# Attention scores in four 32-row groups instead of two 64-row groups, and a two-trip loop written out, in a one-core decoder layer

## The reference

```
inter  = einsum('bhcd,bhde->bhce', qi * q_decay, kv)
scores = einsum('bhcd,bhsd->bhcs', qi, ki) * dmask
intra  = einsum('bhcs,bhse->bhce', scores, vi)
kv_new = r_C * kv + einsum('bhcd,bhce->bhde', ki * k_decay, vi)
```

## Time and profile before

| | |
|---|---|
| median of 3 runs | 180.23 us (179.91 to 180.83) |
| profiled execution, first to last instruction (span) | 178.7 us |
| PE busy | 152.3 us (85%) |
| DVE busy | 126.4 us (71%) |
| ACT busy | 61.8 us (35%) |
| POOL busy | 35.9 us (20%) |
| mean granted TensorE clock | 0.971 |

### The profile page before, as it was taken

The page is one execution under the profiler, slowest core; times in us unless marked ns, Lnnn a source line. Parts: engine busy times, 40 slices in busy tenths (PEclk is TensorE's granted clock), DMA queues, the critical chain, the costliest instruction groups (busy, mean ns, idle before and its releaser), DMA issues.

```text
span 178.7 us, 3036 instructions
## 1 busy us (share of the span) xinstructions
PE 152.3 (85%) x983; PEld 106.6 (60%) x983; DVE 126.4 (71%) x396; ACT 61.8 (35%) x171; POOL 35.9 (20%) x54
## 2 busy tenths in 40 slices
PE   0399964797997999999959999999599889998991
PEld 0267433573662678867626888677258757745880
DVE  0633599647487995975789959757899565877762
ACT  3346880103487132054751320547613220311110
POOL 3104163013161002222410013125100113010020
PEclk9999996569999999999999999999999999999999
DMA  5999200000200000000004000000010000001001
GB/s 173 290 360 340 57 0 4 0 0 2 69 10 0 0 4 0 0 2 0 0 4 132 0 0 0 0 0 0 0 59 0 4 2 0 0 0 59 4 0 59
DMA packets 7930, 7.29 MB, mean 41 GB/s; under 512 B 2264, under 2 KB 7664, under 8 KB 7792
## 3 DMA queue, kind: packets, MB, share of 16 engines
q1 hardware_dynamic: 7424, 6.79, 12.1%
q10 hardware_dynamic: 496, 0.37, 0.7%
HBM read 6.11 MB, written 1.05 MB: 40 GB/s over the span
## 4 chain that ended last, share of the span: by engine, by line
PE 43%; DVE 33%; issue 7%; ACT 6%; DVEq 5%; POOL 3%; DMA 2%; POOLq 0%
PE bank L784 15%; PE ebank L784 11%; DVE probs L613 9%; PE bank L894 4%; POOL rs L325 3%; DVE b_e_parts L738 3%; DVE stats L519 2%; ACT qx L425 2%; PE ebank L792 2%; DMA xin<-in_x 2%; DVE norm L530 2%; DVEq L520 2%; PE bank L799 2%; DVE acc L557 2%; PE bank L890 1%
## 5 line engine op out<-in xcount | busy, mean ns | idle before, releaser
L613 DVE TENSOR_TENSOR probs<-bank,dec 128x512 f32<-128x512 f32 x32 | 19.8, 683 | 1.9 <-PE bank L852 1.9
L852 PE MATMUL bank<-qx,kT 64*128 64x512 f32 x64 | 18.4, 625 | 0.7 <-ACT kv L480 0.7
L325 POOL TENSOR_TENSOR rs<-ve,nhalf 128x2 f32<-128x2 f32 x16 | 11.4, 711 | 36.6 <-DVE ve L524 36.5
L877 PE MATMUL bank<-probs,vpad 128*32 128x128 f32 x256 | 10.8, 293 | 4.1 <-DVE probs L613 4.1
L799 PE MATMUL bank<-cst,norm 128*128 128x128 f32 x36 | 6.4, 301 | 9.1 <-DVE norm L530 9.1
L784 PE MATMUL ebank<-w_e_hi,h3T_hi 128*128 128x512 f32 x40 | 13.3, 413 | 0.0
L557 DVE SCALAR_TENSOR_TENSOR acc<-ebank,gate,acc 128x256 f32<-128x256 f32 x26 | 11.3, 477 | 2.5 <-PE ebank L784 2.3
L425 ACT ACTIVATE qx<-bank,cst 128x256 f32<-128x256 f32 x32 | 12.6, 489 | 0.0
L557 DVE SCALAR_TENSOR_TENSOR acc<-bank,gate,acc 128x256 f32<-128x256 f32 x22 | 9.3, 478 | 4.5 <-PE bank L784 3.0
L784 PE MATMUL ebank<-w_e_hi,h3T_lo 128*128 128x512 f32 x40 | 12.5, 393 | 0.0
L784 PE MATMUL ebank<-w_e_lo,h3T_hi 128*128 128x512 f32 x40 | 12.4, 392 | 0.0
(11 more groups left out here) (135 smaller groups left out, 332.8 us busy)
## 6 DMA issues: line engine op xcount, KB each, us to landing
w_e<-in_L_ffn_We SPq DMA_DIRECT2D x2, 1024.0 KB, 10.8
xin<-in_x SPq DMA_DIRECT2D x4, 256.0 KB, 3.6
dec<-in_decay SPq DMA_DIRECT2D x1, 1024.0 KB, 7.9
out<-outb SPq DMA_DIRECT2D x8, 128.0 KB, 1.7
cst<-in_consts ACTq DMA_DIRECT2D x1, 282.0 KB, 3.6
w_qkv<-in_L_attn_Wq SPq DMA_DIRECT2D x1, 256.0 KB, 4.2
w_qkv<-in_L_attn_Wk SPq DMA_DIRECT2D x1, 256.0 KB, 4.6
w_qkv<-in_L_attn_Wv SPq DMA_DIRECT2D x1, 256.0 KB, 4.9
```

Source lines behind the costliest of these rows:

```text
L325: nc.gpsimd.tensor_tensor(dst[:], src[:], nhalf[:], ALU.pow).then_inc(done, 1)
L613: nc.vector.tensor_tensor(probs[:, t, 4 * n:4 * n + 4, :], bank[2 + n][:].rearrange("p (h n) -> p h n", h=4), dec[:, 4 * n:4 * n + 4, :], ...
L852: pe.matmul(bank[2 + n][:], kT[rows, t, g, :], qx[rows, t, g, :, :], start=True, stop=True).then_inc(s_sc_ps, 1)
L877: mm = pe.matmul(bank[t][32 * q:32 * q + 32, g * P:(g + 1) * P], vpad[:, t, h, :], probs[:, t, h, :], start=(par == 0), stop=(par == 1 and ...
```

## The change

The four row groups of the array that hold two heads each take the place of the two that hold four. `qx` has two masked copies (even and odd heads) instead of four. A product of `scores` takes 32 rows of kT and 256 columns of `qx`, and there are eight for a tile: for g = 0 one from each row group q into the left half of bank 2+q, then for g = 1 into the right half. The semaphore steps only after the g = 1 product of a bank, and `scores(1)` waits for bank 2+q ahead of its g = 0 product. A bank so holds heads of both groups; the decay table is permuted to match, and `attend` reads `probs` through the new order and takes all its waits in its first four products. Apart from that the loop of passes 2 and 3 is written out, and a dummy product of 512 columns becomes two of 256.

```diff
@@ shape_constants
-    c[:, C_PICK:C_BLOCK] = (head_of_row[:, None] % 4) == np.arange(4)[None, :]
+    c[:, C_PICK:C_BLOCK] = (head_of_row[:, None] % 2) == np.arange(2)[None, :]
...
-    decay = np.where(diff[:, None, :] >= 0, r[None, :, None] ** np.maximum(diff, 0)[:, None, :], 0.0)
+    order = [g * 8 + q * 2 + a for q in range(PAIRS) for g in range(GROUPS) for a in range(2)]
+    decay = np.where(diff[:, None, :] >= 0, r[None, order, None] ** np.maximum(diff, 0)[:, None, :], 0.0)
@@ decoder_layer
-        qx = sb("qx", [P, TILES, GROUPS, 4, P])
+        qx = sb("qx", [P, TILES, GROUPS, 2, P])
@@ passes
-            with eng.Fori(2, B) as i:
+            for i in range(2, B):
                 body(i, True, True, True)
@@ head_queries
-                    for k in range(4):
+                    for k in range(2):
                         o = act.activation(qx[:, t, :, k, :], bank[t][:, 0:D].rearrange("p (g n) -> p g n", g=GROUPS),
                                            ACT.Copy, scale=cst[:, C_PICK + k:C_PICK + k + 1])
@@ keep_clock
-                for _ in range(n):
-                    pe.matmul(dst[:], ident, cst[:, 0:512], start=True, stop=True)
+                for _ in range(2 * n):
+                    pe.matmul(dst[:, 0:256], ident, cst[:, 0:256], start=True, stop=True)
@@ scores
                     for g in range(GROUPS):
-                        for half in range(2):
-                            n = 2 * g + half
-                            if t > 0:
-                                pe.wait_ge(s_sc, QUADS * (TILES * i + t - 1) + n + 1)
-                            rows = slice(64 * half, 64 * half + 64)
-                            pe.matmul(bank[2 + n][:], kT[rows, t, g, :], qx[rows, t, g, :, :],
-                                      start=True, stop=True).then_inc(s_sc_ps, 1)
+                        for q in range(PAIRS):
+                            if t > 0 and g == 0:
+                                pe.wait_ge(s_sc, QUADS * (TILES * i + t - 1) + q + 1)
+                            rows = slice(32 * q, 32 * q + 32)
+                            mm = pe.matmul(bank[2 + q][:, g * D:(g + 1) * D], kT[rows, t, g, :],
+                                           qx[rows, t, g, :, :], start=True, stop=True)
+                            if g == GROUPS - 1:
+                                mm.then_inc(s_sc_ps, 1)
@@ attend
-                                h = g * 8 + q * 2 + par
-                                if h % 4 == 0:
-                                    pe.wait_ge(s_sc, QUADS * (TILES * i + t) + h // 4 + 1)
-                                mm = pe.matmul(bank[t][32 * q:32 * q + 32, g * P:(g + 1) * P], vpad[:, t, h, :],
-                                               probs[:, t, h, :],
+                                if g == 0 and par == 0:
+                                    pe.wait_ge(s_sc, QUADS * (TILES * i + t) + q + 1)
+                                mm = pe.matmul(bank[t][32 * q:32 * q + 32, g * P:(g + 1) * P],
+                                               vpad[:, t, g * 8 + q * 2 + par, :],
+                                               probs[:, t, (q * GROUPS + g) * 2 + par, :],
                                                start=(par == 0), stop=(par == 1 and t == 0))
```

More of the change, by code:

```diff
@@ L50 @@
 C_PICK = C_QDEC + GROUPS * P
-C_BLOCK = C_PICK + 4
+C_BLOCK = C_PICK + 2
 C_IOTA = C_BLOCK + P
@@ L256, in decoder_layer, with passes @@
         block = stack.enter_context(nc.Block())
-        def passes(eng, body):
+        def passes(body):
             body(0, True, False, False)
             body(1, True, True, False)
-            with eng.Fori(2, B) as i:
+            for i in range(2, B):
                 body(i, True, True, True)
@@ L307, in body @@
                         sp.dma_start(out[b].rearrange("(t p) d -> p t d", p=P)[:, t, :], outb[:, t, :]).then_inc(done, 16)
-            passes(sp, body)
+            passes(body)
             sp.wait_ge(s_st0, 16 * B)
@@ L363, in body @@
                     rsqrt(rms_rs, rms_ve, i, s_rms_var, s_rms_rstd, TILES)
-            passes(pool, body)
+            passes(body)
         @block.scalar
@@ L507, in body @@
                     act.copy(biases[:], bank[1][:].rearrange("p (t n) -> p t n", t=TILES)).then_inc(s_gb_sb, 1)
-            passes(act, body)
+            passes(body)
         @block.vector
@@ L770, in body @@
                 assert (not front or vf.n == vf.each) and (not back or vb.n == vb.each), (vf.n, vb.n)
-            passes(dve, body)
+            passes(body)
         @block.tensor
@@ L1023, in body @@
                         expert_unit(j, u)
-            passes(pe, body)
+            passes(body)
 _INS = ["x", "ctx_512", "L0_attn_Wq", "L0_attn_Wk", "L0_attn_Wv", "L0_attn_Wo", "L0_attn_rms_w",
```

## The result

| | before | after |
|---|---|---|
| median (lowest to highest), 4 runs each | 180.5 us (179.91 to 180.83) | 187.91 us (185.25 to 190.07) |
| profiled execution, device time | not shown | 188.58 us |
| its span | 178.7 us | 186.3 us |
| mean granted clock | 0.971 | 0.888 |

The change made the kernel slower: ratio 1.032, interval 1.025 to 1.039. Forecast were 178.7 us and a range up to 180.2, so both the size and the direction were wrong. The forecast was taken off a median of three runs, 180.23 us; the table has a fourth. The ratios in this document leave out runs that were more than 1.5% above the fastest of the same kernel (two of the four after, six of the ten of experiment 2, two of the four of experiment 6, one of the eight of experiment 14), while medians, mean spans and mean clocks are taken over all runs. By the ratio the change costs 5.8 us, by the medians 7.4.

The account below looks back on a forecast made before the run. The chain was taken as PE (43%) and DVE (33%) handing over to each other, ACT mattering at few places. Gains of 0.74 + 0.8 = 1.54 us off 180.23 gave 178.7 us; own range 178.2 to 179.4, overall 176.4 to 180.2.

Parts of the forecast that it names:

- The scores on PE: Scores products of both tiles: `scores(0)` shortens inside a gap, `scores(1)` stays covered by DVE's work; gain and cost 0.
- the clock falls in passes 1 to 3: Rival: shorter `scores(0)` lengthens PE's gap to 2.4 us, clock falls; about 3.2 us a pass, 181.9 to 188; chance 0.13.
- The masked copies, pass 0: Two fewer ACT copies start `w_e_lo` sooner and let `b_e_parts` go sooner; gain 0.74 us.
- `ez`, passes 1 to 3: Two fewer ACT copies ahead of `ez` end DVE's wait for it; gain 0.8 us over three passes.
- `scores(0)` on PE: Tile 0's 16 records run four side by side, taking 1.1 us instead of 1.99; nothing gained, as a gap covers it.
- The waits of `scores(1)`: Tile 1's first bank is ready at 97.5, DVE wants it at 97.66; cost 0, with 0.1 to 0.2 us to spare.
- The attend tail: `attend(1)` ends 0.70 us later, absorbed by PE's 0.62 us wait for the gates; cost 0, at worst 0.1 us a pass.
- The loop written out: Passes 2 and 3 without the loop: register work saved on all engines, counted as 0.
- the clock in pass 0: Rival: PE's clock in pass 0 doesn't fall or returns sooner; up to 2.5 us more gain, 176.2 to 178.2; chance 0.15.
- The sum: All terms together: 0.74 + 0.8 = 1.54 us gained, span 177.2 us, median 178.7 us.

Follow-up runs that it names:

- experiment 2: Changed kernel with two dummy products of 256 columns behind `scores(0)` in passes 1 to 3: 182.82 us, ratio 1.0046 to the kernel before.
- experiment 6: Changed kernel with tile 0 back in the old form and tile 1 new: 190.8 us, ratio 1.0438 to the kernel before.
- experiment 14: Changed kernel with the four g = 0 products of `scores(1)` on all 128 rows in all passes: 179.71 us, ratio 0.9979 to the kernel before.
- experiment 10: Experiment 6 with the four g = 0 products of `scores(1)` on all 128 rows instead of 32: 179.77 us, ratio 0.999 to the kernel before.
- experiment 4: Kernel before with `scores(0)` of passes 1 to 3 cut to 256 of its 512 columns, rows left at 64: 181.25 us, ratio 1.0048.
- experiment 5: Changed kernel with tile 0 new and tile 1 back in the old form: 179.35 us, ratio 0.9958 to the kernel before.
- experiment 1: Kernel before with only the loop of passes 2 and 3 written out and each 512-column dummy split in two: 180.93 us, ratio 1.0036.
- experiment 8: Changed kernel with full-row dummies behind `scores(0)` and behind the first three g = 0 products of `scores(1)`: 184.0 us, ratio 1.0213 to the kernel before.
- experiment 9: Kernel before with `attend` taking all four waits in its first four products: 180.15 against 180.13 us, ratio 1.0006.
- 11: Experiment 6 with each bank's g = 0 and g = 1 products of `scores(1)` issued in a row: 182.89 us.
- Experiment 12: Changed kernel with tile 1 new in pass 0 alone, the loop kept, 512-column dummies behind `scores(0)`: 177.58 us, ratio 0.9881 to the kernel before.
- experiment 7: Experiment 5 with full-row dummy products behind `scores(0)` in passes 1 to 3: 179.73 us, ratio 0.9953 to the kernel before.

## Why the prediction was wrong

**The step that failed** is "The scores on PE". It asked whether the time of the products was covered, found that it was, and put their price at 0. The price of `scores(1)` was not its time but what it did to the clock: 9.2 us over three passes in the profiled execution. Experiments 10 and 14 give nearly all of it back by the rows of four products alone (ratio 1.032 for the change, 0.998 for experiment 14).

**The rival that came true** is "the clock falls in passes 1 to 3". Its size was good, with some luck: 3.2 us a pass and 188 us were worked out, and 9.2 us over three passes and 187.91 us came, but as 5.1, 2.0 and 2.1 us, and the ratio of 1.032 alone would make it 186.3 us. Its mechanism was half right. I blamed a shorter `scores(0)` and a longer gap, and gave it 0.13 because "the gap stays well under that of pass 0, and products follow it at once". Both were true, and beside the point. The gaps of 2.43 us in experiment 4 and 2.25 in experiment 5 brought short falls in some passes and cost 1 us or less. Pass 1 of the changed kernel lost most (5.1 us) behind a gap of only 1.44. I had counted the time that PE was busy, in which a 32-row product counts as much as a full one. The Trainium skill ("TensorE: Matmul & The Clock Gate", HAM oscillation) puts a fall down to idle stretches between bursts of products, as I had. This case's runs agree for the short falls at most, which in experiments 1, 4 and 5 and in pass 3 of 14 came behind gaps of 1.6 to 2.4 us (those of experiment 8 came behind 0.33 to 0.37). They do not agree for the fall that cost the time: with 0.81 us idle ahead, experiment 6 fell to 0.50 and experiment 10 stayed at 1.00.

**The masked copies, pass 0: right where it was sized, but little of it arrived.** `w_e_lo` starts at 23.09 (23.68 before; 0.14 of it is the start of this execution, whose L426 stands at 19.97 where L425 stood at 19.83), `b_e_parts` ends at 27.89 and the projection starts at 33.27 instead of 33.86. PE's first norm of pass 1 then stands at 42.20 against 42.46, so that 0.26 us is left of the 0.59. TensorE was granted 0.50 from 34 to 38 us in both executions, and in that of the change already from 26 to 30 us, against 0.78 before. That this is what ate the gain is not shown.

**`ez`, passes 1 to 3: right, and sized a little low.** The reciprocal L605 no longer waits. From the first norm of pass 1 to its third the changed kernel takes 15.04 us against 15.34, and the stretches on to the norms of passes 2 and 3 are 0.51 and 0.54 shorter. Some 0.3 us of that is the written-out loop (experiment 1), which leaves about 1.0 us against 0.8. So the 1.6 us of the table are 0.26, 1.0 and 0.3 us, where the forecast had 0.74, 0.8 and 0. The sum came out by luck.

**`scores(0)` on PE: right.** 1.15 us for 16 records, 1.1 forecast, so the 32-row products did run side by side. (The 0.43 us for a pass of two half-array products should have been 0.45: 1.99 less 0.2, over four.)

**The waits of `scores(1)`, "0, with 0.1 to 0.2 us to spare": right as long as the clock holds.** In pass 1 of experiment 6 decay starts 0.33 us behind `state`, as before. In the changed kernel, where the clock falls within this stretch of pass 1, it is 0.42 us (60.81 and 61.23).

**The attend tail: right.** Absorbed by the wait for the gates (experiment 9).

**The loop written out, "0": right for the mean span, mis-sized outside it**, where it added 0.3 to 0.5 us.

**The rival "the clock in pass 0" did not come true in the changed kernel's profile**, but it did in some of the others. In experiment 14 the same stretch reads

```profile
34.00:38.00 4.00, 4.00 (x22) 3.56 (x22) 1.98 (x7) 0.00 (x0) 0.69 (x1) 1.00 0.00 0
```

where the kernel before and the changed one have 0.50, and the third norm of pass 1 stands at 55.98 us, against 57.80 before.

**The sum.** With the great fall gone (experiment 14) the span was 177.5 us in the profiled execution and 177.9 in the mean, against 177.2, and the time 179.71 us against 178.7. That this is near is in part cancelling: up to the third norm of pass 1 this execution is 1.8 us ahead of the kernel before, where the changed kernel was 0.56 ahead, and pass 3 lost 1.3 us behind a short fall. The gains were of the right size in sum; the forecast fell over one resource that it had not priced.

**What stays open.** How rows and spread combine: bank by bank (11) is milder with the same rows, and three full-row dummies (8) did not hold the clock. Neither was taken further. In experiment 10 the 16 records also end 0.3 us later, and no run separates that from the rows. Why a short fall comes in one pass and not in the next, behind the same gap (experiment 4), is open too. Experiment 12's last 1.1 us were not taken apart by a run. In the profiled executions the third norm of pass 1 stands at 55.70 us there and at 56.69 in experiment 7, and TensorE was granted 1.00 from 34 to 38 us against 0.73, so the lead is there by then; how much of it is the clock is not shown.

## What to carry to other kernels

When a change makes TensorE's work narrower (fewer rows for each product, in the same stretch of time), price the clock of what stands behind it, not only the time of the products: read the granted clock there, and work out what that stretch would cost at the lower level. Here narrow products were cheap where they ran in one dense burst, as in `scores(0)`, and dear where waits spread them over microseconds, as in `scores(1)`. Take such a change apart by tile or by pass, for the half that gains may be kept alone (177.58 against 180.13 us here).

## What the runs showed of the hardware that was not expected

- With number, columns, order and waits unchanged, the rows of four products for each tile 1 set the granted clock: mean 0.903 at 32 rows, 0.971 at 64, 0.984 at 128. With the rows left at 32 and the order changed to bank by bank it was 0.944.
- In experiment 6 the clock fell inside a stretch in which PE was busy for 4.00 of 4.00 us (56 to 60, granted 0.96, then 0.50). A busy PE in the profile is no sign that the clock will hold. The same 16 records fill 2.70 us in `scores(1)`, where they wait for DVE, and 1.15 us in `scores(0)`.
- Gaps of 2.4 us ahead of 64-row products were followed by 1.00 in one pass and by a fall that ended within 4 us in the next (experiment 4). One of 1.44 us ahead of 32-row products was followed by 12 us at 0.50.
- The loop written out left the span alone (178.31 against 178.36 us in the mean) and added 0.5 us outside it in experiment 1, 0.3 us in the others.
